# Flamingo block with routed experts: gathered rows split on ScalarE and GpSimd and turned by SyncE's DMA transposes, a fifth chunk's shared steps ahead of the routed blocks, stores issued by ScalarE

## What is computed

```python
x = x + tanh(g_xattn[0]) * cosine_attention(layernorm(x), ctx_768, Wv, bv, Wt, bt)
x = x + tanh(g_ffn[0]) * ffn(layernorm(x), ...)

# ffn, for the 4096 rows xf
shared_out = silu(xf @ shared_w1) * (xf @ shared_w2) @ shared_w3
scores = sigmoid(xf @ router_w)
_, top_idx = top_k(scores + expert_bias, 2)
for w1, w2, w3, g in experts:            # g is 0 for the rows that did not choose it
    routed_out += (silu(xf @ w1) * (xf @ w2) @ w3) * g
```

## Time and profile before

| | us |
|---|---|
| median of 3 runs | 559.43 (558.39 to 563.18) |
| the profiled execution's own time | 562.16 |
| its span, from the first to the last instruction | 560.4 |
| outside the span | 1.8 |
| PE busy | 533.4 (95% of the span) |
| DVE busy | 401.7 (72%) |
| ACT busy | 307.7 (55%) |
| POOL busy | 248.8 (44%) |

### The profile page before, as it was taken

The page is one execution under the profiler, slowest core; times in us unless marked ns, Lnnn a source line. Parts: engine busy times, 40 slices in busy tenths (PEclk is TensorE's granted clock), DMA queues, the critical chain, the costliest instruction groups (busy, mean ns, idle before and its releaser), DMA issues.

```text
span 560.4 us, 13037 instructions
## 1 busy us (share of the span) xinstructions
PE 533.4 (95%) x4164; PEld 346.6 (62%) x4164; DVE 401.7 (72%) x896; ACT 307.7 (55%) x592; POOL 248.8 (44%) x242
## 2 busy tenths in 40 slices
PE   5998999999899999994999999999999999999997
PEld 2566778565565656662666666666666656566564
DVE  0276798957987777772888888888888647677775
ACT  3424777683246566640777777777777733233332
POOL 3000332335147777875444433444443045666770
PEclk9969899999999999997999999999999999999999
DMA  7996576639206020102233333333344122374442
GB/s 184 308 381 225 180 231 228 211 130 316 76 0 208 8 89 0 39 0 60 80 111 109 110 100 103 114 105 105 100 108 100 58 90 80 96 243 128 138 142 83
DMA packets 53437, 72.55 MB, mean 129 GB/s; under 512 B 8049, under 2 KB 43441, under 8 KB 53377
## 3 DMA queue, kind: packets, MB, share of 16 engines
q1 hardware_dynamic: 44192, 51.75, 28.5%
q0 software_dynamic: 8608, 17.91, 11.6%
q10 hardware_dynamic: 576, 2.10, 1.1%
HBM read 49.64 MB, written 22.09 MB: 128 GB/s over the span
## 4 chain that ended last, share of the span: by engine, by line
PE 69%; POOL 13%; DVE 6%; issue 5%; DMA 4%; ACT 2%; SPq 1%; DVEq 0%; ACTq 0%; POOLq 0%
PE bank L1480 17%; PE bank L1576 17%; POOL slot_token L551 13%; PE bank L1501 9%; PE bank L1602 8%; PE bank L1586 4%; PE bank L1560 3%; DMA X<-in_x 3%; PE bank L1375 2%; PE bank L1341 2%; PE bank L1355 1%; PE bank L1363 1%; PE bank L1345 1%; PE bank L1388 1%; ACT WR L623 1%
## 5 line engine op out<-in xcount | busy, mean ns | idle before, releaser
L1480 PE MATMUL bank<-XTC,WS 128*128 128x512 f16 x768 | 176.3, 379 | 1.6 <-DVE WS L927 1.0
L1480 PEld LDWEIGHTS bank<-XTC,WS 128*128 128x128 f16 x768 | 74.7, 98 | 80.4 <-DVE WS L927 1.3
L568 POOL DMA_INDIRECT ROWS<-xrow,idx x72 | 77.2, 1073 | 96.2 <-PE bank L1560 82.8
L1576 PE MATMUL bank<-WR,XTB 128*64 x432 | 100.2, 381 | 0.5 <-DVE STAGE L1223 0.4
L1576 PE MATMUL bank<-STAGE,XTB 128*64 128x512 f16 x432 | 100.2, 381 | 0.0
L585 POOL DMA_INDIRECT ROWS<-yrow,posi x64 | 63.8, 997 | 55.0 <-DMA yrow<-ROWS 26.8
L551 POOL DMA_INDIRECT slot_token<-tokid,sloti x64 | 72.2, 1129 | 34.9 <-issue 19.2
L795 ACT ACTIVATE STAGE<-WR 128x1024 f16 x72 | 76.8, 1066 | 18.5 <-PE bank L1602 17.9
L717 ACT ACTIVATE SIL<-bank 128x512 f32<-128x512 f32 x63 | 37.6, 597 | 81.9 <-PE bank L1480 80.7
L1576 PEld LDWEIGHTS bank<-WR,XTB 128*64 128x64 f16 x432 | 44.7, 110 | 43.7 <-issue 7.2
L1115 DVE SCALAR_TENSOR_TENSOR G<-bank,SIL 128x512 f32<-128x512 f32 x63 | 43.4, 689 | 28.9 <-ACT SIL L717 28.2
(11 more groups left out here) (171 smaller groups left out, 853.2 us busy)
## 6 DMA issues: line engine op xcount, KB each, us to landing
WR<-in_routed_w SPq DMA_DIRECT2D x39, 256.0 KB, 4.4
yrow<-ROWS SPq DMA_DIRECT2D x72, 128.0 KB, 1.7
X<-in_x SPq DMA_DIRECT2D x4, 1024.0 KB, 14.4
xrow<-STAGE SPq DMA_DIRECT2D x8, 512.0 KB, 4.9
xtd<-STAGE SPq DMA_DIRECT2D x8, 512.0 KB, 3.0
out<-X SPq DMA_DIRECT2D x7, 512.0 KB, 3.1
WR<-in_shared_w SPq DMA_DIRECT2D x3, 1024.0 KB, 12.9
WR<-in_ctx_t SPq DMA_DIRECT2D x3, 768.0 KB, 10.3
```

Source lines behind the costliest of these rows:

```text
L568: pool.indirect_dma_start(out=XG[:, u, :], out_offset=None, in_=xrow, in_offset=bass.IndirectOffsetOnAxis(ap=idx[:, b:b + 1].bitcast(U32), ...
L1480: last = pe.matmul(acc[:, :], WS[:, wx, at:at + P], XTC[:, u, xx, k, :], start=(k == 0 and m == 0), stop=(k == KD - 1 and m == 2))
L1576: last = pe.matmul(bank[u][part, :], XTB[:, b % 4, xx, k, part], w[s], start=(k == 0 and m == 0), stop=(k == KD - 1 and m == 2), tile_posi ...
```

## The change

1. **Rows split as they lie, then turned by DMA.** The fp32 transposes on PE (L1560) are gone. ACT writes the high half of the gathered rows straight from `XG` into a staging place, `halves(b)` (`x_hi`); POOL writes the low half (`x_lo`, until now DVE's work); and SP issues one DMA transpose a block (`turn_block`), which writes the 128 x 512 fp16 values, turned, into `XTB`. The staging place is a slot of `YS` for the blocks 0 to 3 and one of two slots of `GS` after that, so `x_hi(b)` waits for the transpose of b-2. POOL's gather of b+4 now stands behind `x_lo(b)` on POOL and waits for it.
2. **All eight steps of the fifth chunk ahead of the blocks.** `NSE` is 40, `CUTS` spreads the weight splits over more steps, and the adds of `TILES` go over the steps 43 to 62.
3. **Stores issued by ACT.** `store_block` stands on ACT, two stores an iteration, each behind DVE's copy of that block. The last two stand in step 40.

```diff
+        XH = [YS[:, b, :].bitcast(F16) for b in range(4)] + [GS[:, 1, u, :] for u in range(2)]
...
-        EX = 4
-        NSE = NSA + EX
+        NSE = NSA + J
...
-        CUTS = [0] * (J + 5) + [2, 1] * 10 + [1] * 2 + [0]
+        CUTS = [0] * (J + 5) + [2, 1] * 6 + [1] * 14 + [0]
         assert len(CUTS) == NSE and sum(CUTS) == 2 * E
-        FIRST, LEFT = NSE + 4, NC * J - 1 - (NSE + 4)
+        FIRST, LEFT = NSE + 3, NC * J - 1 - (NSE + 3)
...
+            def turn_block(b):
+
+                u = b % 4
+                sp.wait_ge(b_xlo, b + 1)
+                if b >= 4:
+                    sp.wait_ge(b_h, b - 3)
+                sp.dma_start_transpose(XTB[:, u, :, :, :].rearrange("p a k n -> p (a k) n"), halves(b))\
+                    .then_inc(xt_in[u], 16)
+
+            for b in range(NRUN):
+                turn_block(b)
...
             def fetch(b):
                 u = b % 4
-                if b >= 4:
-                    pool.wait_ge(b_tx, b - 3)
...
+            def x_lo(b):
+                u = b % 4
+                pool.wait_ge(b_xhi, b + 1)
+                pool.tensor_tensor(halves(b)[:, D:2 * D], XG[:, u, :], halves(b)[:, 0:D], ALU.subtract).then_inc(b_xlo, 1)
+
+            for b in range(4):
+                fetch(b)
             for b in range(NRUN):
-                fetch(b)
+                x_lo(b)
+                if b + 4 < NRUN:
+                    pool.wait_ge(b_xlo, b + 1)
+                    fetch(b + 4)
...
+            def x_hi(b):
+                u = b % 4
+                act.wait_ge(xg[u], 16 * (b // 4 + 1))
+                if b == 4:
+                    act.wait_ge(s_y, NSE)
+                elif b >= 6:
+                    act.wait_ge(xt_in[(b - 2) % 4], 16 * ((b - 2) // 4 + 1))
+                act.activation(halves(b)[:, 0:D], XG[:, u, :], ACT.Copy).then_inc(b_xhi, 1)
...
+                if n == NSE - 1:
+                    x_hi(0)
+                    x_hi(1)
                 silu(n, n % J)
...
+            def store_block(b):
+                u = b % 4
+                act.wait_ge(b_yev, b + 1)
+                act.dma_start(yrow[b * P:(b + 1) * P, :], YS[:, u, :]).then_inc(st_y[u], 16)
...
                 if b + 4 < NRUN:
                     x_hi(b + 4)
                     x_hi(b + 5)
-                odd_second(b + 1, w, b == 0)
+                if b > 0:
+                    store_block(b - 2)
+                    store_block(b - 1)
+                    odd_second(b + 1, w)
...
-            def x_lo(b):
-                dve.wait_ge(b_xhi, b + 1)
-                dve.tensor_tensor(XTB[:, b % 4, 1], XB[b % 2][:, 0:KD * P].rearrange("p (k n) -> p k n", k=KD),
-                                  XTB[:, b % 4, 0], ALU.subtract).then_inc(b_xlo, 1)
...
             def block_hidden(b, e):
                 u = b % 2
-                pe.wait_ge(b_xlo, b + 1)
+                pe.wait_ge(xt_in[b % 4], 16 * (b // 4 + 1))
...
                 hidden_transpose(b)
                 hidden_transpose(b + 1)
-                if b + 4 < NRUN:
-                    block_transpose(b + 4)
-                    block_transpose(b + 5)
```

More of the change, by code:

```diff
@@ L319, in flamingo_block @@
         xg = [sem(f"xg{i}") for i in range(4)]
-        b_tx = sem("b_tx")
+        xt_in = [sem(f"xt_in{i}") for i in range(4)]
         b_xhi = sem("b_xhi")
@@ L464, in _ @@
             load_raw(E - 1)
[L466 to L478, removed]
+            def turn_block(b):
[7 more added lines that the diff above has]
+                turn_block(b)
+            sp.wait_ge(s_h, (NC - 2) * J)
+            sp.dma_start(XTC[:, LAST % 2, :, :, :].rearrange("p a k n -> p (a k n)"),
+                         xtd[LAST * P:NC * P, :]).then_inc(ld_xtc[LAST % 2], 16)
             for c in range(LAST):
@@ L769, in _ @@
                                   xtd[(c + 2) * P:(c + 3) * P, :]).then_inc(ld_xtc[c % 2], 16)
[L771 to L776, removed]
             def r_silu(b, u, first=False):
@@ L795, in odd_second @@
                 act.activation(W3[:, b % 2], odd_half(w, b)[:, :, W3E:WE], ACT.Copy).then_inc(odd_w3, 1)
-            act.wait_ge(s_g, NSE)
-            x_hi(0)
-            x_hi(1)
+            x_hi(2)
+            x_hi(3)
             act.wait_ge(routed_ok, 1)
             act.wait_ge(w_lo, 2 * E)
+            w = act.value_load(blk_word[0:1, ds(NW, 1)])
+            odd_second(0, w, True)
+            odd_second(1, w, True)
             for b in range(0, NRUN, 2):
@@ L804, in _ @@
                 r_silu(b + 1, 1, b == 0)
[L805 to L810, removed]
+                if b > 0:
+                    if b % 4 == 0:
+                        w = act.value_load(blk_word[0:1, ds(NW + b // 4, 1)])
+                    odd_second(b, w)
                 g_hi(b, 0, b == 0)
@@ L820, in _ @@
                 silu(n, n % J)
+                if n == NSE:
+                    store_block(NRUN - 2)
                 hidden_hi(n, n % J)
+                if n == NSE:
+                    store_block(NRUN - 1)
             n, a = NC * J - 1, (J - 1) % 2
@@ L1082, in block_words, with add_shared @@
                 dve.tensor_copy(blk_word[:, :], bank[6][0:1, 0:PARTS * NW]).then_inc(routed_ok, 1)
-            def add_shared(c, combined=None, steps=J):
-                dve.wait_ge(s_y, c * J + steps)
+            def add_shared(c, combined=None):
+                dve.wait_ge(s_y, c * J + J)
                 if combined is not None:
@@ L1226, in _ @@
             w = dve.value_load(blk_word[0:1, ds(NW, 1)])
-            x_lo(0)
             odd_first(0, w, True)
-            x_lo(1)
             odd_first(1, w, True)
-            add_shared(NCA, steps=EX)
+            add_shared(NCA)
             for b in range(0, NRUN, 2):
@@ L1240, in _ @@
                     odd_first(b + 3, w)
-                if b == 0:
-                    x_lo(2)
-                    x_lo(3)
-                else:
+                if b > 0:
                     rows(b - 2)
@@ L1248, in _ @@
                 g_lo(b + 1, 1)
-                if b + 4 < NRUN:
-                    x_lo(b + 4)
-                    x_lo(b + 5)
             dve.wait_ge(b_tg, NRUN)
@@ L1262, in _ @@
                 gate_hidden(n, n % J)
-                if n % J == 1:
+                if n % J == 1 and n // J - 1 > NCA:
                     add_shared(n // J - 1, combined=2 * done)
@@ L1501, in shared_rows @@
                         last = pe.matmul(acc, GATED[n % 3][gx][:, i * P:(i + 1) * P], WS[:, wx, at:at + D],
-                                         start=(n in (NSE, n - j) and m == 0 and i % 2 == 0),
-                                         stop=((j == J - 1 or n == NSE - 1) and m == 2),
+                                         start=(j == 0 and m == 0 and i % 2 == 0),
+                                         stop=(j == J - 1 and m == 2),
                                          skip_group_check=True)
@@ L1552, in weights @@
                     .rearrange("p a n -> p (a n)")
-            def block_transpose(b):
-                slot = b % 4
-                pe.wait_ge(xg[slot], 16 * (b // 4 + 1))
-                if b >= 2:
-                    pe.wait_ge(b_xlo, b - 1)
-                for k in range(KD):
-                    last = pe.transpose(XB[b % 2][:, k * P:(k + 1) * P], XG[:, slot, k * P:(k + 1) * P], ident[:, :])
-                last.then_inc(b_tx, 1)
             def block_hidden(b, e):
                 u = b % 2
-                pe.wait_ge(b_xlo, b + 1)
+                pe.wait_ge(xt_in[b % 4], 16 * (b // 4 + 1))
                 pe.wait_ge(odd_w12, b + 1)
@@ L1627, in _ @@
                 hidden_transpose(b + 1)
-                if b + 4 < NRUN:
-                    block_transpose(b + 4)
-                    block_transpose(b + 5)
-            hidden(NSE, NCA % 2, EX)
+            hidden(NSE, (NCA + 1) % 2, 0, load=(NCA + 1) // 2 * 16 + 16)
             block_rows(NRUN - 2, es[NRUN - 2 - LAST_WORD])
-            hidden(NSE + 1, NCA % 2, EX + 1)
+            hidden(NSE + 1, (NCA + 1) % 2, 1)
             block_rows(NRUN - 1, es[NRUN - 1 - LAST_WORD])
```

12 lines of the change are left out of this document (5 added, 7 removed).

## The result

The changed kernel takes 589.81 us (median of 4 runs, 589.21 to 591.32) against 560.17 for the kernel before on the same chip: a ratio of 1.052, 95% interval 1.048 to 1.056. The forecast was 542, with a range to 570. It is slower, on the side of the rival with 0.17. Some executions of a kernel run a few per cent longer at a lower granted clock; the ratios here leave them out, the medians don't.

A forecast was written before the change was run, and what follows sets the result against it. The prediction took PE to bound the kernel, above all in the blocks. Its terms, -7.8 + 3.2 - 15.6 + 2.9 = -17.3 us, against the median of 559.43 gave 542 us, with a range from 532 to 570.

The forecast's parts named there:

- the rival with 0.17: In the blocks, PE waits for slow transposes: 575 us (0.12) or far above, about 682 (0.05); chance 0.17.
- What bounds the kernel: Whole kernel: mostly PE; in the blocks nothing but PE, 5.04 us a pair without a gap.
- Part 1: The blocks: without PE's fp32 transposes, 35 pair intervals of 4.8 us, 168.0 us in place of 175.8, -7.8 us.
- The landing L: In the blocks, time from issue to landing of a DMA transpose, taken as 2.35 to 2.4 us.
- the forecast's own formula: In the blocks, pair interval is 3.55 us plus half a transpose's landing time, with PE's floor at 4.60 us.
- ACT's two issues: In the blocks, two stores issued by ACT ahead of `odd_second` cost 0.05 us a pair, up to 0.66.
- the case near 740 us: In the blocks, a block's four squares turned one behind another: 5.2 us a block, 10.5 a pair.
- the one near 682: In the blocks, SP's queue handles a transpose only after the one before landed: 8.8 us a pair, 308 us; chance 0.05.
- Part 2: Four steps moved ahead of the blocks: hidden(2) starts 3.2 us later, four steps behind the blocks go, -15.6 us.
- Part 3: Behind the blocks, POOL's 64 gathers and last adds set the end: +2.9 us given back.
- The rival of late gathers: Behind the blocks, POOL's gathers stall as before, 12.1 us of waiting for DVE's adds: up to 554 us; chance 0.05.
- The third: In the blocks, PE waits for `xt_in`; slower overall from 5.3 us a pair, a landing of 3.5 us; chance 0.17.

The follow-up runs named there:

- e1_steps8: The kernel before with all eight steps of the fifth chunk ahead of the blocks, PE's transposes kept: 555.66 us, ratio 0.991.
- e2_steps6: The kernel before with six steps of the fifth chunk ahead of the blocks in place of four: 550.02 us, ratio 0.980.
- e7b_idle: The kernel before with one added DMA transpose a block between scratch places that nobody reads: 562.78 us, ratio 1.001.
- e6b_copy: The changed kernel with a plain DMA copy in place of the transpose from block 4 on: block products 187.2 us against 212.3.
- e3_slots4: The changed kernel with four staging slots for the split rows in place of two: 585.3 us.
- e4_stores_sp: The changed kernel with the block stores back on SP's queue, ahead of the transposes: 577.46 us.
- e5b_early: The changed kernel with four staging slots, stores on SP, and the high halves written some 2 us earlier on ACT: 560.31 us, ratio 0.998.
- f2_dve: The changed kernel with four staging slots, stores on SP, earlier high halves, and low halves written by DVE: 605.25 us, ratio 1.066.

## Why the prediction was wrong, point by point

**What bounds the kernel** held: with PE's own transposes the blocks took 179.6 to 179.8 us, whatever changed around them (e1_steps8, e2_steps6, e7b_idle).

**Part 1 failed, in three steps.**
- *The landing L.* It was taken at 2.35 to 2.4 us, the middle of the store's and the gather's; it is 3.7 (2.4 to 6.0). With 3.7 the forecast's own formula gives 3.55 + 1.85 = 5.4 us a pair, 189 us, +13 and not -7.8. e6b_copy shows that it is the turning: a copy at the same place lands in 2.1. And e7b_idle has it as long beside the old kernel's traffic. The nearest rows were moves of whole rows, and the bound of 4.4 from a small load was nearer the truth than the middle.
- *The staging slot.* `x_hi(b+5)` waits for the transpose of b+3, and the forecast left this wait out of its list though it names it among the edits. It put the landing time into ACT's queue, in front of the stores, the weight copy and the silus. The formula had one path for L; there were two. From 5.4 to the measured 6.0 us a pair 0.6 us are missing, 21 us in all. That this wait and ACT's queue make them up is only partly shown: the slots alone gave 5 us of the stretch (e3_slots4), the stores alone 9 (e4_stores_sp); both with an earlier `x_hi` gave 29 (e5b_early), but an earlier `x_hi` shortens the forecast's own path as well. A rival was not tested: the blocks wait for the late landings and not for the median. The 15 on the chain take 3.5 to 6.0 us, 4.9 in the mean, and with L = 4.9 the forecast's formula gives 3.55 + 2.45 = 6.0 by itself. So L is the term that failed for certain; how the last 0.6 us part between the spread of L and the second path stays open.
- *ACT's two issues.* Priced at 0.05 us a pair, with 0.66 as the bound. They hold ACT's queue for 0.83 us, and ACT stands idle for 0.71 us between `x_hi` and the weight copy; idle time of this kind ahead of the weight copies is 28.3 us in all. The row from which the price was read the earlier trace rows had an activation running over one issue; here ACT had just waited, so only one `x_hi` of 0.42 us lay over two. e4_stores_sp: 9 us over 35 pairs, 0.25 us each.

POOL's subtraction (0.73 us), the gather behind it, `x_hi` at 0.42 and DVE's slack were right.

Against the two prices of the Trainium skill: its page "Advanced Engine Details and Errata", section X-Bar Transpose (TRN2), has transposing DMAs as fast as regular ones. The traces do not agree for 128 x 512 fp16 within SBUF: 3.7 us to landing against 2.1 for the copy. The Trainium skill's page "VectorE: DVE Perf Modes", section The three transpose paths, gives 1309 ns for one 128x128 square by DMA. Four squares landed in 3.7 us and two in 3.3, and held the queue for 1.19 and 1.17, so here squares did not go one behind another at that price, and the case near 740 us fell. So did the one near 682: the transpose that SP issued at 305.6 us landed at 310.7, and SP had issued the next one at 309.9.

**Part 2 was nearly right.** +5.8 in place of +3.2: the first transpose landed 4.85 us after its issue and not 2.4, POOL's first subtraction took 1.14 us, and PE stood idle for 1.11 us in front of hidden(0). Without the DMA path it was +3.6 (e1_steps8).

**Part 3 was right in kind.** The end became POOL's. Given back were 15.6 - 11.9 = 3.7 us after a forecast of 2.9, and 15.6 - 9.5 = 6.1 in e1_steps8, where the adds and gathers take turns too. The rival of late gathers, at 0.05, was partly true there. e2_steps6 leaves 26 steps for them and gets all 7.8 us.

**The rivals.** The third, PE's wait for `xt_in` with L over 3.5 us, is what came; its price at L = 3.7 would have been 189 us in the blocks and a net of about +4. Its chance of 0.17 was too small: the landing of 4.4 us stood among the rows and was set down as an end, and neither the spread of the landings nor the second path, which made even a median of 3.7 us dear, was in the formula. A range ending at 570 left it out.

## What to carry to other kernels

Price a DMA that turns data by itself, not from copies of the same bytes, and ask for every wait that it brings where the waiting engine's queue stands, not only when its result is wanted: here the slot that it frees held up ACT and with it the silus. Put late landings and not the middle one into a loop that waits for each. Where a part of a change fills an idle stretch, try it alone and in other sizes: six steps ahead of the blocks in place of four brought 2%, all eight brought 1%, since they moved the bound to POOL's gathers. On a queue in order, put what a chain waits for ahead of what nobody waits for.

## What the runs showed of the hardware that was not expected

- A DMA transpose of 128 x 512 fp16 within SBUF lands 2.4 us after its issue at best and 3.7 in the median beside one gather and one store a block; a copy of the same bytes in 2.1. It holds SP's queue for 1.19 us (copy 0.47), and half the size holds it for 1.17.
- It takes about 1.0 us of all 16 DMA engines (e7b_idle), and as long as nobody waits for it it costs the kernel nothing: 68 of them changed the time by a ratio of 1.001.
- In f2_dve, with PE idle for 1.1 to 4.4 us about once in two pairs of blocks, the granted clock was a mean of 0.86 over 140 us, and the same products took 4.40 us in place of 2.71. In the kernel before, the stretch with the 7.94 us idle time has a mean of 0.73 (window, its length, PE, PEld, DVE, ACT and POOL busy with their counts, the granted clock, DMA share, GB/s):

```profile
252.00:264.50 12.50, 4.88 (x28) 3.15 (x28) 1.99 (x4) 0.77 (x2) 7.08 (x8) 0.73 0.20 56
```
